# A differential-attention and mixture-of-experts block: the sixteen shared tiles side by side from slot 8 to 38, identity products in all pairs of slots that hold no tile and in the lead

## The reference

```python
xn = _layernorm(x)
x = x + attention(xn) + ffn(xn)

# attention: 8 heads of 16, each with two maps of 8 features
scores = jnp.einsum('bqhif,bkhif->ibhqk', qs, ks_) * scale
atts = jax.nn.softmax(scores, axis=-1)
att = atts[0] - diff_weight * atts[1]
o = jnp.einsum('bhqk,bkhe->bqhe', att, vs)
rms = jax.lax.rsqrt(jnp.mean(o * o, axis=(-2, -1), keepdims=True) + eps)
out = ((o * rms * norm_w).reshape(b, s, e) @ Wo.T + bo) * (1.0 - diff_weight)

# ffn: a shared expert for all tokens, the best 2 of 8 routed experts, 128 -> 256 -> 128
shared = jax.nn.silu(xf @ Ws1) * (xf @ Ws3) @ Ws2
h = jax.nn.silu(jnp.einsum('td,edf->tef', xf, We1)) * jnp.einsum('td,edf->tef', xf, We3)
routed = jnp.einsum('tef,efd,te->td', h, We2, w)
out = (shared + routed) / (N_SHARED + TOP_K)
```

## Time and profile before

| | us |
|---|---|
| median of 3 runs | 660.99 (656.55 to 661.47) |
| the profiled execution | 660.85 |
| its span, first to last instruction | 658.8 |
| PE busy in it | 632.3 |
| DVE busy | 481.4 |
| ACT busy | 413.4 |
| POOL busy | 219.5 |
| mean granted clock of TensorE | 0.916 |

### The profile page before, as it was taken

How to read it: one execution, slowest core, us unless ns; L and a number is a source line. 1 busy time by engine, 2 the same in 40 slices (tenths; PEclk the granted TensorE clock), 3 DMA queues, 4 the chain that set the end, 5 groups by cost and what they waited for, 6 DMA issues and landing times.

```text
span 658.8 us, 13172 instructions
## 1 busy us (share of the span) xinstructions
PE 632.3 (96%) x4501; PEld 352.5 (53%) x4501; DVE 481.4 (73%) x1012; ACT 413.4 (63%) x808; POOL 219.5 (33%) x296
## 2 busy tenths in 40 slices
PE   7799999999999999999999999999999999999995
PEld 6445434545454344365666665656556656655553
DVE  4999667867786576677777787777777787776374
ACT  4543456655664556677777777777677766677662
POOL 5620053554454453022323232233323242333000
PEclk9667769987996679799999999999999999999998
DMA  6975202240141302547245734746344725220741
GB/s 171 204 135 115 72 28 48 62 98 22 35 93 31 88 26 82 125 129 209 87 150 129 216 105 132 182 137 188 120 109 121 233 80 172 81 71 17 209 134 49
DMA packets 62529, 74.04 MB, mean 112 GB/s; under 512 B 7296, under 2 KB 42496, under 8 KB 62464
## 3 DMA queue, kind: packets, MB, share of 16 engines
q1 hardware_dynamic: 57952, 64.00, 37.4%
q0 software_dynamic: 4352, 8.95, 4.0%
q10 hardware_dynamic: 160, 0.26, 0.2%
HBM read 40.08 MB, written 15.80 MB: 85 GB/s over the span
## 4 chain that ended last, share of the span: by engine, by line
PE 82%; DVE 7%; issue 5%; ACT 3%; POOL 1%; DMA 1%; SPq 0%; POOLq 0%; DVEq 0%; ACTq 0%
PE O L1114 19%; PE ST L1097 17%; PE F L1152 11%; PE F L1165 8%; PE ST L1102 7%; PE F L1149 4%; DVE rowmax L809 3%; PE S L1078 3%; PE F L1132 2%; PE F L1047 2%; ACT probs L626 1%; PE O L988 1%; PE F L1063 1%; PE F L1004 1%; PE F L1038 1%
## 5 line engine op out<-in xcount | busy, mean ns | idle before, releaser
L809 DVE TENSOR_REDUCE rowmax<-S 128x1 f32<-128x512 f32 x486 | 313.6, 684 | 94.2 <-PE S L1078 86.3
L626 ACT ACTIVATE probs<-ST 128x512 f32<-128x512 f32 x490 | 266.0, 595 | 144.5 <-PE ST L1102 131.1
L1097 PE MATMUL ST<-qop,kop 32*128 32x512 f32 x490 | 147.1, 521 | 6.1 <-ACT probs L626 4.9
L1078 PE MATMUL S<-kop,qop 32*128 32x512 f32 x486 | 147.1, 526 | 2.4 <-DMA kop<-kparts 0.9
L1114 PE MATMUL O<-probs,vop 128*32 128x512 f32 x1024 | 138.2, 652 | 0.0
L460 POOL DMA_INDIRECT yt<-ysb,xst x72 | 72.3, 1004 | 147.3 <-DMA yt<-ysb,xst 137.3
L1097 PEld LDWEIGHTS ST<-qop,kop 32*128 32x128 f32 x490 | 59.1, 190 | 111.5 <-ACT probs L626 73.7
L1102 PE MATMUL ST<-mop,ones_r 2*128 2x512 f32 x490 | 117.8, 433 | 0.0
L449 POOL DMA_INDIRECT xs<-xn,slot_i x64 | 62.9, 983 | 74.9 <-DVE rowmax L809 59.8
L1152 PEld LDWEIGHTS F<-xsT,wrt_all 128*128 128x128 f32 x576 | 69.7, 191 | 26.0 <-issue 26.0
L1152 PE MATMUL F<-xsT,wrt_all 128*128 128x128 f32 x576 | 83.4, 288 | 0.0
(11 more groups left out here) (154 smaller groups left out, 608.1 us busy)
## 6 DMA issues: line engine op xcount, KB each, us to landing
wrt_all<-in_wexp SPq DMA_DIRECT2D x72, 384.0 KB
qop<-qparts SPq DMA_DIRECT2D x64, 128.0 KB
kop<-kparts SPq DMA_DIRECT2D x62, 128.0 KB
xs<-xst SPq DMA_DIRECT2D x12, 387.0 KB, 6.5
xst<-xs SPq DMA_DIRECT2D x36, 129.0 KB
base<-in_x SPq DMA_DIRECT2D x8, 256.0 KB, 4.7
xn<-yt SPq DMA_DIRECT2D x8, 256.0 KB, 4.8
out_x<-base SPq DMA_DIRECT2D x7, 256.0 KB, 3.3
```

Of the source, the lines that this page charges most:

```text
L626: A(probs[:, n % NP, :], st_bank(n)[:, :], ACT.Exp, scale=SCALE).then_inc(s_p, 1)
L809: V.reduce_max(rowmax[hf][:, (k + 2) % BANDS, q // QT % HC, q % QT:q % QT + 1], s_bank(n)[:, :], AX).then_inc(s_mx, 1)
L1078: mm(s_bank(n)[:, :], qop[b % 2][at:at + BAND, c, t * P:(t + 1) * P], kop[b % 2][at:at + BAND, c, :], start=True, stop=True, tile_position ...
L1097: mm(st_bank(n)[:, :], kop[b % 2][at:at + BAND, c, t * P:(t + 1) * P], qop[b % 2][at:at + BAND, c, :], start=True, stop=False, tile_positi ...
```

## The change

`SH_AT` becomes 8, 10, ... 38. The tiles of slots 0 and 2 and of 116, 120 and 124 leave their places; pairs 16, 22, 28, 32 and 36 get one. `bare(slot)` is true for a slot from 0 to 127 whose pair has no tile: slots 0 to 7, 40 to 43 and 116 to 127. Each of these gets an identity block in step 1 and in step 3: 12 products up to slot 7 and 7 elsewhere, in F[0], but F[1] in slots 4 and 5. The blocks of 6 go. In the lead, 12 products follow each slot's score tiles except in slot -9 (F[0] in slots -11 and -10, F[2] after), and 12 more (F[2]) the small tasks of slots -8 to -3. In all 608 products come (120 + 72 in the lead, 192 in slots 0 to 7, 56 in 40 to 43, 168 in 116 to 127) and 84 go.

```diff
--- before.py
+++ after.py
@@ -56,7 +56,7 @@
 
     LEAD = 11
     RT_AT = [44 + 2 * r for r in range(RT_TILES)]
-    SH_AT = [0, 2, 8, 10, 12, 14, 18, 20, 24, 26, 30, 34, 38, 116, 120, 124]
+    SH_AT = [8 + 2 * i for i in range(SH_TILES)]
     TILE_AT = sorted(SH_AT + RT_AT)
     LOAD_Y0 = RT_AT[-1] + 5
     COMBINE_AT = [LOAD_Y0 + 2 + b for b in range(BATCH - 1)] + [SLOTS - 1]
@@ -92,6 +92,9 @@
         if slot % 2 == 0 or even >= SLOTS or tile_at(even) is not None:
             return even, 1
         return (even, 3) if even % 4 == 0 else (even + 1, 1)
+
+    def bare(slot):
+        return 0 <= slot < SLOTS and tile_at(slot - slot % 2) is None
 
     def rest(slot):
         return 3 if slot >= 0 and slot % 2 == 0 else 1
@@ -1205,6 +1208,8 @@
                     if slot < 0 and k == 0:
                         for i in range(4):
                             score_max(slot + LEAD, i)
+                        if slot != -9:
+                            keep_busy(12, 0 if slot < -9 else 2)
                     if slot >= 0 and k % 2 == 1:
                         for i in (k - 1, k):
                             if slot < SLOTS:
@@ -1215,8 +1220,8 @@
                         for i in (k - 1, k):
                             if slot < SLOTS:
                                 subtract_max(slot, i)
-                    if k == 1 and RT_AT[-1] < slot < SLOTS and slot % 4 in (2, 3):
-                        keep_busy(6, 0)
+                    if k == 1 and bare(slot):
+                        keep_busy(12 if slot < 8 else 7, 1 if slot in (4, 5) else 0)
                     for i in (slot - 2, slot - 1):
                         if 0 <= i < SLOTS and weigh_at(i) == (slot, k):
                             weigh(i)
@@ -1236,6 +1241,8 @@
                         if x is not None:
                             do_xT(x)
                         other(slot)
+                        if -9 < slot < -2:
+                            keep_busy(12, 2)
                         if slot == -1:
                             keep_busy(28, 2)
                         if slot == END:
@@ -1247,8 +1254,8 @@
                             do_z(Z_AT.index(slot))
                         if slot - 1 in Z_AT:
                             turn_z(Z_AT.index(slot - 1))
-                        if RT_AT[-1] < slot < SLOTS and slot % 4 in (2, 3):
-                            keep_busy(6, 0)
+                        if bare(slot):
+                            keep_busy(12 if slot < 8 else 7, 1 if slot in (4, 5) else 0)
                         r = routed(tile_at(slot + 1))
                         if r is not None:
                             do_xsT(r)
```

## The result

The changed kernel takes 636.78 us (median of 4 runs, 636.41 to 637.5), the one before 660.92 (4 runs, 656.55 to 661.47): a ratio of 0.9638, 95% interval 0.9590 to 0.9686. The forecast was 636. The profiled execution took 637.5 us, its span is 635.3, 23.5 less than the 658.8 of before.

A forecast was written before the change was run, and what follows sets the result against it. The prediction took TensorE to bound the kernel, before slot 44 partly at half clock. Its terms summed to -25.4 us: 660.85 - 25.4 = 635.5, given as 636, with a range of 627 to 648 us.

The forecast's parts named there:

- Slots 8 to 39: With a shared tile in every pair at full clock: -2.2, -6.2 and -6.3 us for slots 8-15, 16-31 and 32-39.
- Slots 0 to 7: Two tiles go, 192 identities come; at full clock 35.8 us against 43.13, -7.3, bounds -11.7 and +11.3.
- near but not ahead: Slots 0 to 7: VectorE needs about 31 us, less without the two tiles, so it does not set the pace.
- never lose the clock by themselves: Pairs with a tile have their matmuls in the gaps where PE waits, so they keep the clock; no size given.
- Slots 40 to 43: 28 identities a pair (2.0 us) replace a tile's 3.2; 19.0 us against 19.54, -0.5, bounds -1.5 and +1.5.
- The lead: Slots -11 to -1: 192 identities fit under VectorE's 30.6 us, a few blocks at half clock; +0.8, bounds -2.0 and +4.
- plain sum: Slots 116 to 127, TensorE-bound: tiles -9.5, blocks of 6 -6.0, blocks of 7 +11.8, together -3.7 us.
- The first: Rival: the clock still falls in places, about 5.6 us each; one gives 641 us, two 647; chance 0.19.
- The fifth: Rival: another engine, VectorE in slots 0 to 11, becomes the bound; about 639 us, counted within the main 0.58.
- The second: Rival: lead gains 1.5 us and blocks in slots 0 to 7 lie wholly in waits; 629 us, chance 0.10.
- third: Rival: the clock holds but no block before slot 44 is hidden; 654 us, chance 0.06.
- fourth: Rival: identities don't raise the clock in lead and slots 0 to 7 and run at half; 668 us, chance 0.07.

The follow-up runs named there:

- tiles_only: Changed kernel with its new tile places but the identity blocks of the kernel before; median 637.53 us, 631.65 to 646.9.
- no_early_blocks: Changed kernel without the blocks of 12 in slots 0 to 7; median 638.35 us.
- blocks_only: Changed kernel with the tiles back at their old places and the new blocks in every bare pair; median 641.02 us.
- no_tail_blocks: Changed kernel without any identity block in slots 116 to 127; median 628.09 us, 627.31 to 641.52.
- bare16_blocks: Changed kernel with the tile of pair 16 moved to pair 40 and four blocks of 7 in slots 16 and 17; median 638.5 us.
- sparse_no_40: Changed kernel with 12 blocks of 7 instead of 24 in slots 116 to 127 and none in slots 40 to 43; median 637.5 us.

## Why the prediction was right

Its first statement, that the clock falls behind bare pairs and a tile in each keeps it, carries most of the time, and for slots 8 to 39 the runs bear it out: tiles_only has them at clock 1.00, and the kernel with pair 16 bare again is about 8 us slower in four executions of five. Term by term (predicted, measured from the windows):

| stretch | predicted | measured |
|---|---|---|
| start, up to the first score tile | 0 | +0.5 |
| lead | +0.8 | +0.05 |
| slots 0 to 7 | -7.3 | -4.3 |
| slots 8 to 15 | -2.2 | -2.2 |
| slots 16 to 31 | -6.2 | -6.0 |
| slots 32 to 39 | -6.3 | -6.3 |
| slots 40 to 43 | -0.5 | -1.15 |
| 44 to 115, and 116 to 127 | -3.7 | -1.0 - 3.1 |

*Slots 8 to 39* came out as summed, because every pair but pair 8 had been seen at full clock before, or one at the same place of a batch.

*Slots 0 to 7* is the term that was mis-sized, by 3.0 us. The step "At full clock a pair holds 4 rounds of 0.67, 4 blocks of 0.80 and 2 weighings" assumed a clock that holds; 12 identities behind each round don't hold it while VectorE is late with the row maxima. With blocks of 20 in slots 0 and 1 it holds, and the stretch takes 36.35 us against the 35.8 of the sum. That VectorE is "near but not ahead" was wrong in slots 0 and 1. And the gain of the stretch was put down to the full clock of the blocks: no_early_blocks has -3.7 of the -4.3 (39.41 against 43.13) with no identity there, and tiles_only -3.55 with none in the lead either. So the two tiles that leave give most of it without any better clock (0.70). The blocks alone, with the tiles still there, give -2.5 (40.66 in blocks_only), and the two don't add.

The sentence that pairs with a tile "never lose the clock by themselves" does not hold in this stretch. Pair 0 had a tile in the kernel before and spent most of its time at half clock (its window):

```profile
53.28:64.80 11.52, 10.86 (x40) 6.10 (x40) 10.40 (x19) 4.94 (x9) 0.00 (x0) 0.65 0.70 159
```

*Slots 40 to 43* were put at 19.0 us, which is not what the prediction's own terms give (19.3 - 2 x (3.2 - 2.0) = 16.9); it was a guess at what lies in waits, and 18.39 was measured. Without the blocks and at full clock these slots took 17.02 (tiles_only), so the blocks cost 1.4 us there.

*The lead* hid its 192 identities, as argued; the +0.8 for blocks at half clock wasn't needed, though the clock did fall at the lead's start, as the prediction feared.

*The tail's* plain sum was right (-4.1 with the two blocks that I counted there though they stood in slot 115). Hardly any of a block was hidden there: 12 blocks less made the tail 5.4 us shorter, 0.45 each, against 0.49.

*Rivals.* The first happened in small, in slots 1 and 2, and costs about 2 us; "a granted clock at half in a stretch of slots 0 to 43" was named as a sign of being wrong, and it came. The fifth happened with it in part, since it is VectorE that is late there. The second, third and fourth did not: the lead gained nothing, and its blocks lie in waits. The two largest errors, slots 0 to 7 (+3.0) and the sum of lead, slots 40 to 43 and tail (-1.8), partly cancel. That the total is nearer than the terms are is in part luck.

## What to carry to other kernels

Where TensorE's clock falls behind thin stretches, spread the work that has no fixed place so that no stretch is thin, and fill with products that nobody reads only where none is left: in these runs 56 of them in four bare slots were worth 6.4 us, and 384 in the lead and slots 0 to 7 4.4, mostly by steadiness (the best execution without them is only 1.5 us behind). Where the engine is full, each filling block costs its whole length, so try fewer; but look at the spread over executions beside the median, since the version without any in the tail was the fastest of all in four of six executions and slower than the changed kernel in two.

## What the runs showed of the hardware

The clock is not decided by the program alone. Identical code with a bare pair 16 took 635.9 us at a mean clock of 0.986 once and 643.4 to 645 at 0.967 to 0.971 four times, and no_tail_blocks had two levels 13.5 us apart. A wait of 0.91 us in bare16_blocks ended 0.4 us before the clock went down, and in no_tail_blocks it went down within one of 1.30 us. But a long wait is not what it takes, nor is one enough: in sparse_no_40 it fell in the bare slots 40 to 43 with no wait over 0.53 us there, while tiles_only kept it through the same wait in the same slots, and in the changed kernel it stayed at full through one of 0.77 us (up to 101.54 us). What sets how likely a fall is, beyond thin work on PE, was not measured. All three falls came in or behind a pair without a tile. Once down, the clock stayed down for 17 us in bare16_blocks and 41 us in no_tail_blocks, through stretches in which PE was busy nearly all the time (14.28 of 14.28 us and 39.72 of 40.72) at half clock. And the clock's mean says little about time: the lead took 32.8 us at 0.64 and 32.7 at 0.84.
